# A Toeplitz tile built on chip, norms one pair sooner, and another order of the last steps

## The reference

```python
k = einsum('ijk,imk->ijmk', hx, hy)          # outer product of two 1-D filters
y = irfft2(rfft2(x, 512) * rfft2(k, 512) / 512)[..., :256, :256]
out = y + x * bias[:, None, None]            # layer 0
scores = einsum('bpsd,bptd->bpst', x, x) / sqrt(256)
red = sum(scores * weights[None], -1, keepdims=True)
y = x + red                                   # layer 1
y_hat = (y - mean) * rsqrt(var + 1e-5)        # over images, rows, columns of a channel
return y_hat * gamma + beta
```

## Time and profile before

| | |
|---|---|
| median of three runs | 941.79 us |
| profiled execution | 941.66 us |
| its span, first to last instruction | 939.9 us |
| TensorE busy | 926.3 us, 99% |
| VectorE busy | 739.7 us, 79% |
| ScalarE busy | 683.7 us, 73% |
| GpSimd busy | 690.9 us, 74% |
| mean granted TensorE clock | 0.997 |
| moved between HBM and the chip | 244.17 MB, 260 GB/s |

### The profile page before, as it was taken

The page is one execution under the profiler, slowest core; times in us unless marked ns, Lnnn a source line. Parts: engine busy times, 40 slices in busy tenths (PEclk is TensorE's granted clock), DMA queues, the critical chain, the costliest instruction groups (busy, mean ns, idle before and its releaser), DMA issues.

```text
span 939.9 us, 18886 instructions
## 1 busy us (share of the span) xinstructions
PE 926.3 (99%) x5314; PEld 812.5 (86%) x5314; DVE 739.7 (79%) x2197; ACT 683.7 (73%) x1154; POOL 690.9 (74%) x590
## 2 busy tenths in 40 slices
PE   8999999999999999999999999999999999999995
PEld 6888888888888888888888888888888888888884
DVE  2678787888788788788787787878887887887887
ACT  4446787787777777777777867877877777777786
POOL 3777777877877877877877877777778777778764
PEclk9999999999999999999999999999999999999998
DMA  7966999999999999999999998999998989999855
GB/s 240 335 162 221 261 258 260 280 271 262 274 266 241 282 284 252 266 288 242 276 290 221 277 306 249 254 279 266 268 284 255 256 267 258 288 258 279 237 170 208
DMA packets 91455, 244.17 MB, mean 260 GB/s; under 512 B 17200, under 2 KB 41904, under 8 KB 83248
## 3 DMA queue, kind: packets, MB, share of 16 engines
q1 hardware_dynamic: 73296, 235.27, 84.3%
q10 hardware_dynamic: 18144, 8.72, 6.6%
HBM read 176.59 MB, written 67.37 MB: 260 GB/s over the span
## 4 chain that ended last, share of the span: by engine, by line
PE 96%; DVE 1%; POOL 1%; DMA 1%; ACT 0%; issue 0%; POOLq 0%; DVEq 0%; ACTq 0%
PE ps_c L703 37%; PE ps_u L703 32%; PE ps_z L703 27%; POOL zl L453 1%; DMA toep_whole<-filters_padded 0%; POOL ul L453 0%; ACT zh L586 0%; DMA filters_padded<-z_sb 0%; DVE z_sb L1055 0%; DVE products L950 0%; DVE z_sb L873 0%; DVE ul L974 0%; DVE z_sb L940 0%; ACT uh L540 0%; ACT z_sb L532 0%
## 5 line engine op out<-in xcount | busy, mean ns | idle before, releaser
L453 POOL TENSOR_TENSOR zl<-z_sb,zh 128x1024 fp32r<-128x1024 f32 x127 | 305.3, 2404 | 138.3 <-ACT zh L586 138.3
L621 ACT ACTIVATE out_sb<-z_sb,shift,gain 128x256 f32<-128x256 f32 x496 | 257.1, 590 | 4.4
L703 PE MATMUL ps_z<-uh,toep 128*128 128x512 f32 x768 | 257.7, 390 | 0.1
L540 ACT ACTIVATE uh<-ps_u 128x1024 fp32r<-128x1024 f32 x128 | 130.3, 1018 | 153.7 <-PE ps_z L703 151.7
L703 PE MATMUL ps_u<-toep,xh 128*128 128x256 f32 x1024 | 241.9, 317 | 0.1
L950 DVE CUSTOM_DVE_ANT_0 products<-z_sb,ps_c 128x256 bf16<-128x256 f32 x504 | 181.5, 416 | 66.1 <-PE ps_c L703 66.0
L703 PE MATMUL ps_c<-zh,wh 128*128 128x512 f32 x504 | 202.8, 402 | 0.4 <-POOL zl L453 0.4
L974 DVE TENSOR_TENSOR ul<-ps_u,uh 128x1024 fp32r<-128x1024 f32 x128 | 152.8, 1194 | 62.9 <-ACT uh L540 62.8
L940 DVE SCALAR_TENSOR_TENSOR z_sb<-x_sb,par,ps_z 128x1024 f32<-128x1024 f32 x128 | 163.6, 1278 | 47.3 <-ACT out_sb L621 40.9
L703 PE MATMUL ps_c<-zh,wl 128*128 128x512 f32 x504 | 197.2, 391 | 0.0
L703 PE MATMUL ps_c<-zl,wh 128*128 128x512 f32 x504 | 196.4, 390 | 0.0
(11 more groups left out here) (94 smaller groups left out, 920.1 us busy)
## 6 DMA issues: line engine op xcount, KB each, us to landing
xt_sb<-xt_in SPq DMA_DIRECT2D x64, 1024.0 KB, 10.0
x_sb<-x_in SPq DMA_DIRECT2D x128, 512.0 KB, 7.0
out<-out_sb SPq DMA_DIRECT2D x124, 512.0 KB, 5.2
w_sb<-wt_in SPq DMA_DIRECT2D x64, 256.0 KB, 5.2
toep_whole<-filters_padded SPq DMA_DIRECT2D x63, 256.0 KB, 6.5
everyone<-partition_moments ACTq DMA_DIRECT2D x62, 128.0 KB, 4.5
out<-z_sb SPq DMA_DIRECT2D x2, 512.0 KB, 2.8
partition_moments<-own ACTq DMA_DIRECT2D x62, 1.0 KB, 8.0
```

What stands on the lines that cost most here:

```text
L453: nc.gpsimd.tensor_tensor(low, z_sb[:, r, h], high.bitcast(F32), ALU.subtract)\
L540: nc.scalar.activation(uh[:, us.slot(2)], u_bank(us)[:, :, :, :], ACT.Copy)\
L621: last = nc.scalar.activation(to[:, k, b], z_sb[:, r, h, k, b], ACT.Identity, bias=shift[:, r, g:g + 1], scale=gain[:, r])
L703: return nc.tensor.matmul(o, a, b, start=start, stop=stop)
```

## The change

1. **First tile on chip.** Channel 0's right tile is no longer read from DRAM. TensorE multiplies the last layer's input with channel 0's weight column, repeated 128 times, so every partition holds the whole raw filter row in PSUM (`ps_z`). Copies put it into `slide`: partitions 0 to 63 at column 127, partitions 64 to 127 at column 63. Six predicated copies then shift each partition by 32, 16, 8, 4, 2 and 1 columns where a bit of its number is set; the bits come into PSUM by another product. A multiplication by a pre-shifted decay from the parameters (390 more columns of 128 fp32) gives the rounded tile, a second one the exact tile. The warm-up before it has 10 products, not 24.
2. **Norms one pair sooner.** LAG_TOTAL goes from 10 to 9 and LAG_NORM from 11 to 10. totals moves from the even to the odd step, after whole_z; gain_and_offset comes at the head of the even step; inverse_deviation is first in GpSimd's even step.
3. **VectorE's order.** In the even step: low_u, gain_and_offset, statistics, reduce_rows, mean_of_partition, whole_z. In the odd step: low_u, reduce_rows, whole_z, totals, statistics.
4. **The end.** TensorE does product_u(126) before product_c(123). The low part of pair 127 is made in two halves, each waited for by itself. GpSimd computes gains and offsets from channel 59 on and norms one block each of pairs 122, 125 and 126; VectorE norms one block each of pairs 126 and 127. Both of the last channels' mean deviations come from a product with the centring matrix. VectorE's last statistics, sums and means are reordered.

```diff
-WARM_FIRST, WARM_LAYER, WARM_TOEPLITZ = 4, 2, 24
+WARM_FIRST, WARM_LAYER, WARM_TOEPLITZ = 4, 2, 10
-LAG_MEAN, LAG_GATHER, LAG_SPREAD, LAG_TOTAL, LAG_NORM = 6, 7, 8, 10, 11
+LAG_MEAN, LAG_GATHER, LAG_SPREAD, LAG_TOTAL, LAG_NORM = 6, 7, 8, 9, 10
...
-            load_first_toeplitz(1, first_s_landed)
             load_first_toeplitz(0, t_landed[0])
...
 # TensorE, after the last layer
+            for i, half in enumerate(HALVES):
+                column = par[:, COL_WO + ORDER:COL_WO + ORDER + 1].broadcast_to([P, P])
+                mm(ps_z[:, i, 0, 0:P], column, hid[:, half], True, True).then_inc(rows_done, 1)
+            pe.wait_ge(rest_landed, 16)
+            mm(ps_c[:, 1, 0, 0:SHIFTS], par[:, COL_BITS:COL_BITS + P], par[:, COL_BITS + P:COL_BITS + P + SHIFTS],
+               True, True).then_inc(bits_ready, 1)
...
 # ScalarE, before its first step
+            act.wait_ge(rows_done, 1)
+            act.wait_ge(slide_clear, 1)
+            for i in range(2):
+                part_of = slice(64 * i, 64 * i + 64)
+                nc.scalar.activation(slide[part_of, SLIDE_FROM[i]:SLIDE_FROM[i] + P], ps_z[part_of, 0, 0, 0:P],
+                                     ACT.Copy).then_inc(slide_low, 1)
...
 # VectorE, before its first step
+            dve.wait_ge(rows_done, 2)
+            for i, width in enumerate((P // 2, P)):
+                part_of = slice(64 * i, 64 * i + 64)
+                nc.vector.tensor_copy(slide[part_of, SLIDE_FROM[i] + P:SLIDE_FROM[i] + P + width],
+                                      ps_z[part_of, 1, 0, 0:width]).then_inc(slid, 1)
+            dve.wait_ge(slide_low, 2)
+            dve.wait_ge(slide_clear, 1)
+            dve.wait_ge(bits_ready, 1)
+            for i in range(SHIFTS):
+                by = 2 ** (SHIFTS - 1 - i)
+                width = SIDE + by - 1
+                mask = ps_c[:, 1, 0, SHIFTS - 1 - i:SHIFTS - i].bitcast(mybir.dt.int32).broadcast_to([P, width])
+                dve.wait_ge(slid, 2 + i)
+                nc.vector.copy_predicated(slide[:, 0:width], mask, slide[:, by:by + width]).then_inc(slid, 1)
+            dve.wait_ge(slid, 2 + SHIFTS)
+            decay = par[:, COL_FIRST:COL_FIRST + SIDE]
+            nc.vector.tensor_tensor(toep[:, 0, 1, 0], slide[:, 0:SIDE], decay, ALU.mult).then_inc(first_sh_ready, 1)
+            nc.vector.tensor_tensor(toep_whole[:, 0, 1], slide[:, 0:SIDE], decay, ALU.mult).then_inc(first_s_ready, 1)
...
 # GpSimd, after its steps
+            inverse_deviation(Step(0, PAIRS - 6))
+            late_gain_and_offset(Step(0, PAIRS - 6))
+            low_z_half(Step(0, PAIRS - 1), 0)
             shift_means(Step(0, PAIRS - 4))
+            low_z_half(Step(0, PAIRS - 1), 1)
+            pool.wait_ge(shift_ready, CH - 2)
+            late_norm(Step(0, PAIRS - 6), 0).then_inc(late_rows_pool, 1)
             inverse_deviation(Step(0, PAIRS - 4))
             late_gain_and_offset(Step(0, PAIRS - 4))
             pool.wait_ge(shift_ready, CH - 1)
             pool.wait_ge(last_means, 1)
-            nc.gpsimd.tensor_scalar(rows, rows, gain[:, r], shift[:, r, g:g + 1], ALU.mult, ALU.add)\
-                .then_inc(late_rows_pool, 1)
+            late_norm(Step(0, PAIRS - 3), 1).then_inc(late_rows_pool, 1)
             inverse_deviation(Step(0, PAIRS - 2))
+            pool.wait_ge(last_shift, 1)
+            late_norm(Step(0, PAIRS - 2), 1).then_inc(last_done_pool, 1)
...
 # ScalarE, after its steps
-            run_steps(act, PAIRS, 2 * UNROLL, LAG_NORM - 1, stage)
+            run_steps(act, PAIRS, 2 * UNROLL, END_STEPS, stage)
+            norm(Step(0, PAIRS - 8))
+            high_z(Step(0, PAIRS - 1))
+            norm(Step(0, PAIRS - 7))
+            norm(Step(0, PAIRS - 6), [1])
+            norm(Step(0, PAIRS - 5))
+            norm(Step(0, PAIRS - 4))
+            norm(Step(0, PAIRS - 3), [0])
...
 # TensorE, late steps and the last pair
+                product_u(st.trail(LAG_U))
                 if st.number() == PAIRS:
                     wait(pe, red_ready, Step(0, PAIRS - 5), 0)
                     product_c(Step(0, PAIRS - 5), ps_c)
-                product_u(st.trail(LAG_U))
...
+            pe.wait_ge(rest_landed, 16)
+            average(CH - 2)
             pe.wait_ge(red_ready, PAIRS - 2)
-            product_c(end[2], ps_u[:, 0], [0], average_first)
-            average_moment(CH - 2)
+            for k in range(BLOCKS):
+                pe.wait_ge(zl_ready, PAIRS + k)
...
 # VectorE, after its steps
+            block_statistics(end[0], 0)
+            whole_z(end[2])
             totals(Step(0, PAIRS - 6))
-            whole_z(end[2])
+            block_statistics(end[0], 1).then_inc(bn_ready, 1)
+            reduce_rows(end[0], ps_u[:, 0])
+            mean_of_partition(before)
             statistics(end[1])
-            reduce_rows(end[0], ps_u[:, 0])
+            squared_deviation(before, 1)
+            dve.wait_ge(averaged, 2)
+            mean_and_variance(before)
+            wait(dve, c_done, end[1], 1)
+            for b in range(PAIR):
+                reduce_block(end[1], ps_c, 0, b)
+            whole_variance(before, 3)
+            reduce_block(end[1], ps_c, 1, 0)
+            reduce_block(end[1], ps_c, 1, 1).then_inc(red_ready, 1)
             statistics(end[2])
...
-            for h, k, b in ((0, 0, 0), (0, 0, 1), (0, 1, 0), (0, 1, 1), (1, 0, 0), (1, 0, 1)):
-                last = norm_rows(final, h, k, b)
-                if b == 1:
-                    last.then_inc(last_done, 1)
+            for h in range(2):
+                for b in range(PAIR):
+                    last = norm_rows(final, h, 0, b)
+                last.then_inc(last_done, 1)
```

More of the change, by code:

```diff
@@ L134, in first_channel, with by_totals @@
         return st.static() and st.channel() == 0
+    def by_totals(vs):
+        return vs.static() and CH - 5 < vs.channel() < CH - 2
     def late(st):
@@ L427, in late_gain_and_offset, with late_norm @@
                 pool.wait_ge(late_gain, turn)
[L428 to L432, removed]
+                if by_totals(vs):
+                    pool.wait_ge(totals_ready, m + 1)
+                    nc.gpsimd.tensor_tensor(offset[:, r], mean_var[:, e, 0:1], gain[:, r], ALU.mult)\
+                        .then_inc(late_scaled, 1)
+                    pool.wait_ge(late_scaled, turn)
+                    nc.gpsimd.tensor_tensor(offset[:, r], chan_column(2, m), offset[:, r], ALU.subtract)\
+                        .then_inc(late_offset, 1)
+                else:
+                    pool.wait_ge(neg_mean_ready, CH - 4 if m == CH - 5 else CH - 3)
+                    nc.gpsimd.tensor_tensor(offset[:, r], neg_mean[:, r], gain[:, r], ALU.mult)\
+                        .then_inc(late_scaled, 1)
+                    pool.wait_ge(late_scaled, turn)
+                    nc.gpsimd.tensor_tensor(offset[:, r], offset[:, r], chan_column(2, m), ALU.add)\
+                        .then_inc(late_offset, 1)
+            def late_norm(no, k):
+                r, h = no.ring(XR), no.half()
+                for b in range(PAIR):
+                    g = (h * BLOCKS + k) * PAIR + b
+                    rows = z_sb[:, r, h, k, b]
+                    last = nc.gpsimd.tensor_scalar(rows, rows, gain[:, r], shift[:, r, g:g + 1], ALU.mult, ALU.add)
+                return last
             def low_toeplitz(ts, part, high, low):
                 t = ts.ring(2)
-                wait_chan(pool, high, ts, 1)
+                if part == 1 and first_channel(ts):
+                    pool.wait_ge(first_s_ready, 1)
+                else:
+                    wait_chan(pool, high, ts, 1 - part)
                 nc.gpsimd.tensor_tensor(toep[:, t, part, 1], toep_whole[:, ts.ring(XR), part],
@@ L742, in product_y, with product_c @@
                 last.then_inc(y_done, 1)
-            def product_c(cs, bank, blocks=range(BLOCKS), between=None):
+            def product_c(cs, bank):
                 wait_chan(pe, wl_ready, cs, 1)
@@ L755, in product_c @@
                         last = mm(bank[:, a], w_l, high[:, k], False, k == BLOCKS - 1)
-                        if between is not None and k == 0:
-                            between(CH - 2)
-                if BLOCKS - 1 in blocks:
-                    last.then_inc(c_done, 1)
-                else:
-                    last.then_inc(c_half_done, 1)
+                last.then_inc(c_done, 1)
             def product_u(us):
@@ L780, in product_u @@
                     mm(o, xl[:, s, b, rows], toep[:, t, 1, 0, :], False, False)
+                    if first and h == b == 0:
+                        pe.wait_ge(first_s_ready, 1)
                     last = mm(o[:, P:SIDE], xt_sb[:, r, PAIR * us.half() + b, 1, rows],
```

257 lines of the change are left out of this document (131 added, 126 removed).

## The result

The changed kernel took 944.26 us (median of 9 executions, 941.93 to 947.37) against 941.87 (941.34 to 942.26) for the kernel before on the same chip: a ratio of 1.003 with an interval of 1.002 to 1.004. So it is slower by 2.4 us, where 2.8 us faster was forecast, and its executions differ by 5.4 us, where those of before differ by 0.9. The profiled execution took 943.86 us, 2.2 more than that of before, for a span of 941.9 us.

What follows compares the result with a forecast made beforehand. TensorE, busy for 99% of the span, was taken as the bound, so time could be won only at start and end: 941.66 - 1.75 - 0.9 = 939.0 us, the loop giving 0; range 937.6 to 941.2.

Steps and rivals of the forecast that it cites:

- Start: Before the first real product: the on-chip tile brings it to 15.05 from 16.78 us, a gain of 1.75 us.
- Loop: Loop over pairs: TensorE stays busy and totals asked a step sooner still have 18.6 us for their transfers; change 0.
- End: After the last products: whole_z of pair 127 starts sooner, fewer VectorE norm rows, earlier stores; 0.8 to 0.9 us gained.
- (a): Start gives little: predicated copies near twice the price, or TensorE's clock drops in its pause; about 940.4 us, chance 0.15.
- (b): Tail gives nothing: VectorE's and GpSimd's norm rows run in turns, 2.5 us in place of 1.4; 939.9 us, chance 0.13.
- (c): Slower loop: in every even step whole_z stands behind GpSimd's shift; 945 us, chance 0.10.

Runs made afterwards that it cites:

- start_alone: The kernel before with only the start's edits, the on-chip first tile; 940.81 us against 941.89.
- start_again: Repeat of start_alone, the kernel before with the on-chip first tile alone, on the chip of after_again; 940.47 us.
- end_back: The changed kernel with the end of before, keeping the new start and loop; 942.87 us, executions 7 us apart.
- older_totals: The changed kernel, with VectorE's totals for channels 1 to 58 reading the transferred moments of the channel before (four buffers in place of two); 941.66 us.
- both_moved: The changed kernel, with ScalarE issuing the first moments transfer sooner in the loop, and the second behind norm and rounding in the end; 940.60 us.
- loop_back: The changed kernel with the lags and the VectorE and GpSimd orders of the loop before, keeping the new start and end; 943.32 us.
- after_again: The changed kernel, unchanged, measured again on another chip than the first; 947.81 us.

## Why the prediction was wrong

**Start: right.** Predicted 15.05 (14.87 and 0.15 are 15.02) for the first product, measured 15.21; the six predicated copies 2.95 us against 2.86, the row products end at 11.04 against 11.05, no fall of the clock in a pause of 1.68 us. First product_y 1.47 us sooner, against 1.75; in the median of the time start_alone and start_again won 1.1 and 1.4 us.

**Loop: this is the step that failed.** The prediction put it so: "from the mean's way out at about 515.9 to the totals of that channel at 534.5 lie 18.6 us, and its two transfers take 8.0 and 4.5 in the median", and so 0. A wait in an in-order queue is set by the slowest of 62, not by the median, and the rows to ask were there: in before the first transfer took up to 10.2 us and the second up to 8.3. No channel had both, though. From the first issue to the second landing lay at most 17.3 us in before, and 16.8 to 19.4 in the other runs with the old loop, against 18.6 to 19.0 of room. So the room was all but used up, and at the latencies of before 0 would still have been nearly right. What made it wrong is that the change itself made the first transfer slower: in the changed kernel the same stretch took up to 21.6 us. I moved the issue without asking what it was moved behind. Slack, from the landing of the second transfer to the totals, was 13.4 us in the median and 8.1 at the least in before; in the changed kernel it is 4.1, and zero five times. Of what was lost, 6.5 us come from totals that follow the issue of the first transfer after 19.0 us and not 25.6 (means; 18.6 was foreseen), and 1.8 from that transfer's mean latency, 9.8 in place of 7.9, which was not.

The waits of the loop cost 2.4 us in the profiled execution, 6.0 in that of end_back (a lead of 1.1 at pair 3, where product_y started at 41.77 against 42.88, and of -4.85 at pair 121), and nothing in older_totals.

**End: the mechanism was right, one engine was left out.** whole_z of pair 127 "starts at 919.3, as its product is done" was the failed step: it waited for a norm on ScalarE, which stood in order behind the issue of the second transfer. I followed the work on VectorE, GpSimd and TensorE and took ScalarE's queue for granted. Its first transfer of this channel landed in 2.7 us in before and in 7.3 in the changed kernel. The rows show what stood ahead of it, first before, then the changed kernel:

```profile
911.17 0.33 ACTq L592 DMA_DIRECT2D partition_moments<-own  x1
...
912.38 0.34 SPq L370 DMA_DIRECT2D out<-out_sb  x1
```
```profile
910.16 0.34 SPq L380 DMA_DIRECT2D out<-out_sb  x1
...
911.07 0.33 ACTq L640 DMA_DIRECT2D partition_moments<-own  x1
```

In before the 512 KB store of a finished pair was issued behind the transfer; with the new end it is issued 0.9 us ahead, and the transfer lands 0.2 us after that store. In end_back, with the old end, it is again issued ahead of the store and takes 2.7 us. So this is the loop's mistake once more: an issue got a large transfer in front of it.
With ScalarE freed, in both_moved, whole_z of pair 127 starts 37.58 us after product_y of pair 121, where the forecast has 37.55, and the tail is 0.8 shorter. That total is as forecast, but its parts are in part luck: the last row sum came 0.34 us sooner where 0.1 was forecast, and the norm rows saved 0.25 (1.78 against 2.03) where 0.67 was.

**The rivals.** (a) did not happen; its "either way about 940.4" holds for the dearer copies only, a fall of the clock by its own price of 2 us gives 941.0. (b), norm rows in turns, would have made 2.5 us of the last rows; they took 1.78, against 4 x 0.34 = 1.36 for VectorE's four alone, so it holds in part, and costs about 0.4. GpSimd's two rows took 1.25 there and 1.09 at 933.21, where VectorE had small operations only. The Trainium skill (SBUF — State Buffer, Who interferes with whom) has one engine blocked for the other's whole instruction where VectorE runs in a two-port mode; full turns would have been 1.36 + 1.09 = 2.45, and the rows show less; whether these instructions run in that mode isn't shown. (c), slower by whole_z behind the shift, had the right sign for a wrong reason: between 27 and 900 us TensorE never waits for whole_z in the changed kernel, only for row sums, and (c) showed only in loop_back. That its 945 lies near the 944.26 is luck. The mechanism that decided was in none of them. The range ended at 941.2.

## What to carry to other kernels

When a result comes back over DMA to an engine that works in order, compare the slack with the longest transfer of the trace and not with the median, and before moving its issue look at which large transfer it will now stand behind. Issue small urgent transfers ahead of large loads and stores, and put an issue that waits for another transfer behind work that others wait for.

## What the runs showed of the hardware

**A small transfer tends to land with the large one ahead of it, on another issuing engine's queue too**: 12.0 us for 1 KB, landing 1.3 us after the 1 MB load issued 0.9 us before. The Trainium skill (DMA: Bandwidth & Descriptors, Queues, rings and completion order) says that each DMA engine goes round between its queues packet by packet. The trace agrees: the small transfer isn't held back until the load is through. From 562.4 to 565.0 us, with xt landing at 569.35, 118 of its 144 packets run between those of SyncE's queue (q10 is ScalarE's queue, q1 SyncE's):

```profile
q1 hardware_dynamic: 168, 1.00, 98.5%
q10 hardware_dynamic: 118, 0.00, 2.6%
```

The time goes into three parts, medians over the loop of before and of the changed kernel: 3.4 and 3.9 us from the issue to the first packet, 2.0 and 3.4 from the first to the last, 2.6 and 1.9 from there to the landing. The part that grew most is the middle one, in which the packets take turns with the load's. Why the last part takes some 2 us no run here shows.

**A rest can cost twice its length.** In end_back TensorE waited 2.18 us for row sums behind late totals. Its row, and the windows after it:

```profile
531.24 0.50 PE L722 MATMUL ps_c<-zh,wh 128*128 128x512 f32 x1 [2.18 <-DVE red L996]
```
```profile
530.00:531.00 1.00, 0.00 (x0) 0.00 (x0) 1.00 (x7) 1.00 (x3) 1.00 (x2) 1.00 0.89 271
531.00:532.00 1.00, 0.76 (x3) 0.67 (x4) 0.19 (x3) 1.00 (x2) 0.96 (x2) 0.93 0.55 162
532.00:533.00 1.00, 1.00 (x3) 0.75 (x3) 1.00 (x3) 0.14 (x1) 0.00 (x0) 0.50 0.80 318
...
535.00:536.00 1.00, 1.00 (x5) 0.78 (x5) 0.12 (x1) 1.00 (x4) 1.00 (x1) 0.86 0.76 217
```

The granted clock fell to 0.50 (1.2 GHz) after the rest and stayed there to 535. From 526.86, the start of a product_y, to that two channels later lie 32.5 us, elsewhere 28.4: 4.1 us for a wait of 2.2. The changed kernel's wait of 1.14 us at 527.23 cost 1.44, and the granted clock stayed at 1.00. The two longest executions of after_again, 951.3 and 953.5 us, have a mean grant of 0.993 and 0.994, the profiled one of 947.1 us 0.997; but another of 947.4 has 0.994 too, and the shortest, 942.1, has 0.995, so the clock doesn't order these times. What made those two so long is open; neither was profiled.
